# The second feed-forward scatters its results to residual rows, and the next stages' keys, values and masks are prepared ahead of its experts

## The chip, the cores and the metric

One core of a Trainium2 chip runs one launch of the kernel. Its time is the device time of that launch in microseconds (us), median of three runs before the change. TensorE does the matrix products and transposes, VectorE (DVE), ScalarE (ACT) and GpSimd (POOL) the elementwise work. SyncE (SP) issues the plain DMAs and GpSimd the indirect ones, which take their row numbers from a tile.

## The reference

Eight residual blocks follow one another over 4 sequences of 512 rows of 128. The change lies in the fourth, a feed-forward with 8 experts where every row goes to one expert and an expert takes 320 rows at most. The fifth, a relu attention against a context of 77 rows, uses its result.

```python
x = x + _L1_xattn_ref(_layernorm(x, axis=-1), ctx_1024, ctx_1024, ...)
x = x + _L1_ffn_ref(_layernorm(x, axis=-1), L1_ffn_gate_w, L1_ffn_gate_b, L1_ffn_w1, L1_ffn_b1, L1_ffn_w2, L1_ffn_b2)
x = x + _L2_xattn_ref(_layernorm(x, axis=-1), ctx_1024, ctx_1024, mask_1xSxS2_ff0, ...)
...
def _L1_ffn_ref(h, gate_w, gate_b, w1, b1, w2, b2):
    logits = x @ gate_w.T + gate_b
    probs = jax.nn.softmax(logits, axis=-1)
    idx = jnp.argmax(probs, axis=-1)
    top_prob = jnp.max(probs, axis=-1)
    pos = jnp.take_along_axis(jnp.cumsum(one_hot, axis=0), idx[:, None], axis=1)[:, 0] - 1
    keep = pos < capacity
    buf = buf.at[idx, safe_pos].add(x * keep[:, None].astype(x.dtype))
    hdn = jax.nn.relu(jnp.einsum('ecd,edf->ecf', buf, w1) + b1[:, None, :])
    eout = jnp.einsum('ecf,efd->ecd', hdn, w2) + b2[:, None, :]
    gathered = eout[idx, safe_pos]
    out = gathered * (top_prob * keep.astype(x.dtype))[:, None]
```

## The kernel before

The residual stays in SBUF as four tiles `Xb[b]`, one for each sequence (512 rows lie on 128 partitions, 4 blocks of 128 columns). Work is cut into units `i`: units 8 to 11 are the attention of the third block, 12 to 15 that of the fifth, 16 to 19 the feed-forward of the sixth, 20 to 23 the attention of the seventh. Each engine runs its own list of instructions in order; the lists come from the same coroutines, interleaved by `weave` with fractions written by hand. An engine waits on counters (`Signal`) that others raise.

Four routings `route(0)` to `route(3)` are interleaved with units 10 and 11 and what follows. A routing normalizes `Xb[b]` into a tile (`slot[8]` or `slot[9]`, part of `PT`), computes the logits, picks an expert, ranks the rows (two small products with `tri` and `ones`) and writes a slot number into `ints` (L1928); GpSimd then scatters the normalized rows, 512 bytes each, with four indirect DMAs into the DRAM buffer `dbuf` (L2251). VectorE also keeps a second number for the way back and the weight `keep` (L1929 to L1938).

`capacity()` runs the experts. SyncE fetches 320 rows of `dbuf` into one of two buffers (L2366, L2368), TensorE transposes them (L821), VectorE copies the transpose to `OC` (L1944, named `turn1`), four products and their relus (L1370 on ScalarE, L1953 on VectorE) follow, then the second product (`down`). VectorE adds the bias from PSUM into `OT` (L1964 and L1966), and SyncE stores 320 rows in the DRAM buffer `dout` (L2374, L2376). On TensorE the order is: transpose and first product of expert x + 1, second product of x.

After the last expert GpSimd gathers the rows of `dout` for each sequence with four indirect DMAs (L2229), two sequences at once and the others after the square roots of units 12 and 13. VectorE adds gathered row times `keep` to `Xb[b]` (L1536) and starts the layer normalization (L1509, L1514, L1517; GpSimd's reciprocal root L2212; L1522 writes `Ht`); TensorE transposes `Ht` (L507) and the unit goes on: query product, scores, ScalarE's relu L1250, VectorE's mask addition L1641, product with the values, L1644 adds to `Xb`. Beside that stand `l2_prepare` (keys and values of the fifth block), the seventh block's mask (L2167, L2169) and `prepare(a3)`, its keys and values (L1554, L1561, L1575).

At the start `dbuf` is filled with zeros from an SBUF tile (2 stores of 640 KB).

Of the kernel before, what the change touches and what calls it, by code (L numbers as in the profile page):

```python
# [8 lines left out]
F32 = mybir.dt.float32  # L9
# [13 lines left out]
CAP = 320  # L23
# [4 lines left out]
ROW = 257  # L28

# [139 lines left out]
def program(nc, A, out):  # L169
    with ExitStack() as ctx:  # L170
# [34 lines left out]
        PT = sb("PT", 10 * 512)  # L205
# [25 lines left out]
        off1 = sb("off1", 32)  # L231
        ints = sb("ints", 32, I32)
        keep = sb("keep", 16)
# [4 lines left out]
        dbuf = nc.dram_tensor("dbuf", (8 * CAP, 128), F32, kind="Internal").ap()  # L238
        dout = nc.dram_tensor("dout", (8 * CAP, 128), F32, kind="Internal").ap()
# [71 lines left out]
        raws1 = [OT[:, 0:512], OT[:, 512:1024]]  # L311
        outs1 = [OT[:, 1024:1536], OT[:, 1536:2048]]
# [54 lines left out]
        def outputs_at(key, r):  # L367
# [4 lines left out]
            if key[0] % 2 == 0:  # L372
# [9 lines left out]
        ex = [signal("exa", 16), signal("exb", 16)]  # L382
        eo = [signal("eoa", 16), signal("eob", 16)]
        gq = [signal(f"gq{b}", 16) for b in range(NB)]
# [23 lines left out]
        route_, glu, mixed, capV, dve2, d3e, masks, gath = (signal("route"), signal("glu"), signal("mixed"), signal("capV"), signal("dve2"),  # L408
                                                             signal("d3e"), signal("masks"), signal("gath"))
# [7 lines left out]
        def x_at(i):  # L417
            kind, b = units[i]
            if kind == "l0x":
                return ld[f"x{b}"].all()  # L420
            if kind == "l1x":
                return comb.at(b)
            if kind == "l2x":
                return gath.at(b)
            return resid.at(i - 4)
# [57 lines left out]
        def ot_free(key):  # L483
# [6 lines left out]
            return ld["zero"].all() if i == 0 else gath.at(3) if i == 20 else (None, 0)  # L490
# [8 lines left out]
        def tensor(e, w):  # L499
# [287 lines left out]
            def route(b):  # L787
# [4 lines left out]
                for t in range(4):  # L792
                    m = e.transpose(PS[:, k, 128 * t:128 * t + 128], slot[8 + b % 2][:, 128 * t:128 * t + 128], ident[:, :])
# [19 lines left out]
            def capacity():  # L813
                w.wait_ge(*ld["l1f"].all())

                def turn1(x):
                    k, free = banks.take(capV, "x", x)
                    w.wait_ge(*free)
                    w.wait_ge(*ex[x % 2].at(x))
                    for n, (s, c) in enumerate(CP):  # L820
                        m = e.transpose(PS[:, k, s:s + c], raws1[x % 2][0:c, 128 * n:128 * n + 128], ident[0:c, 0:c])  # L821
# [680 lines left out]
        def vector(e, w):  # L1502
# [24 lines left out]
            def norm(i):  # L1527
                kind, b = units[i]
                if kind == "l2x":
                    G = OT[:, 512 * b:512 * b + 512]  # L1530
                    w.wait_ge(*gq[b].all())
                    w.wait_ge(*route_.at("r", b, "w"))
                    w.wait_ge(*resid.at(8 + b))
                    for t in range(4):
                        x = Xb[b][:, 128 * t:128 * t + 128]
                        m = e.scalar_tensor_tensor(x, G[:, 128 * t:128 * t + 128], keep[:, 4 * b + t:4 * b + t + 1], x, ALU.mult, ALU.add)  # L1536
                    m.then_inc(*gath(b))
                    yield
# [335 lines left out]
            def route(b):  # L1874
                H = slot[8 + b % 2]
# [5 lines left out]
                yield from layernorm(Xb[b], H, 2, ("r", b), resid.at(8 + b), sc1[b - 2].all() if b >= 2 else (None, 0))  # L1881
# [3 lines left out]
                L, W8 = v4(R[:, 0:32]), v4(R[:, 32:68])[:, :, 0:8]  # L1885
# [18 lines left out]
                e.reciprocal(P1[:, 4:8], P1[:, 0:4]).then_inc(*route_(*key, 9))  # L1904
# [13 lines left out]
                e.tensor_tensor(C, psl2, v4(off1[:, :]), ALU.add)  # L1918
# [15 lines left out]
                w.wait_ge(*route_.at(*key, "kept"))  # L1934
                kp = keep[:, 4 * b:4 * b + 4]
                e.tensor_reduce(kp, W8, AX, ALU.add).then_inc(*route_(*key, 15))
                w.wait_ge(*route_.at(*key, 15))
                e.tensor_tensor(kp, kp, P1[:, 4:8], ALU.mult).then_inc(*route_(*key, "w"))  # L1938

            def capacity():  # L1940
# [16 lines left out]
                def down(x):  # L1957
                    yield
                    o, k = outs1[x % 2], banks.of(capV, "o", x)
# [4 lines left out]
                    e.tensor_tensor(o[:, 0:256].rearrange("p (t d) -> p t d", t=2), PS[:, k, 0:256].rearrange("p (t d) -> p t d", t=2),  # L1964
                                    bb.rearrange("p (o d) -> p o d", o=1).broadcast_to((128, 2, 128)), ALU.add)
                    e.tensor_tensor(o[0:64, 256:384], PS[0:64, k, 256:384], bb[0:64, :], ALU.add).then_inc(*capV("o", x))  # L1966
# [240 lines left out]
        def gpsimd(e, w):  # L2207
# [14 lines left out]
            def gather(b):  # L2222
                w.wait_ge(*route_.at("r", b, "back"))
                w.wait_ge(*eo[0].all())
                w.wait_ge(*eo[1].all())
                w.wait_ge(*capT.at(7))
                for t in range(4):
                    c = 512 * b + 128 * t
                    e.indirect_dma_start(OT[:, c:c + 128], None, dout,  # L2229
# [3 lines left out]
            def norm(i):  # L2233
                kind, b = units[i]
                if kind == "l2x":
                    yield
# [572 lines left out]
```

## Time and profile before

| | us |
|---|---|
| median of 3 runs | 1205.91 |
| lowest, highest | 1205.54, 1206.64 |
| profiled execution, its own time | 1202.0 |
| its span | 1200.2 |
| TensorE busy | 942.1 (78%) |
| VectorE busy | 609.6 (51%) |
| ScalarE busy | 436.9 (36%) |
| GpSimd busy | 217.0 (18%) |
| mean granted TensorE clock, of full | 0.857 |

The profiled execution lies 0.3% under the median; a difference worked out on its rows is added to the median. Times in rows are microseconds from the start of the span. A row of the timeline merges neighbours of the same kind (x4): its second number runs from the start of the first to the end of the last. What stands in square brackets is the idle time of the engine just before, and what ended it. A GpSimd row of an indirect DMA shows the building of descriptors, the data move later.

### The profile page before, as it was taken

The page shows a single profiled execution, that of the slowest core. Times are in us where ns is not written, and L with a number is a line of the kernel's source. Part 1 is how long each engine was busy: PE and PEld are TensorE (multiplying, and loading weights), DVE is VectorE, ACT ScalarE, POOL GpSimd, SP SyncE. Part 2 cuts the span into 40 slices and gives each one's busy share as a digit, 9 for nine tenths or more (in the row PEclk, how much of TensorE's full clock was granted, in tenths as well). Part 3 has the DMA queues.
Part 4 walks back from the last instruction along what each step waited for, and adds up shares of the span by engine and source line. Part 5 has one row for each costly group of instructions (what it writes and reads, how often), then busy time and mean ns, then how long its engine had stood idle before and what let it go on. Part 6 is the DMA issues. An engine that isn't in the chain of part 4 may idle for free.

```text
span 1200.2 us, 15387 instructions
## 1 busy us (share of the span) xinstructions
PE 942.1 (78%) x5738; PEld 507.2 (42%) x5738; DVE 609.6 (51%) x1637; ACT 436.9 (36%) x750; POOL 217.0 (18%) x214
## 2 busy tenths in 40 slices
PE   4777866597767677479389888887989899888888
PEld 2334444364323333257256423333334334344656
DVE  5344653233545443423553443447687777772534
ACT  2333323142233223011132233233676676565233
POOL 1100050504142101200621010011010000200444
PEclk8889887798978667689689888896999899898999
DMA  9600001212036100011200100000000000102030
GB/s 289 230 1 1 1 28 43 68 54 79 22 121 193 34 1 7 23 42 45 55 2 7 36 1 1 1 1 1 2 1 2 1 1 2 36 2 67 32 91 17
DMA packets 41200, 49.18 MB, mean 41 GB/s; under 512 B 5817, under 2 KB 30674, under 8 KB 40488
## 3 DMA queue, kind: packets, MB, share of 16 engines
q1 hardware_dynamic: 36328, 39.15, 10.6%
q0 software_dynamic: 4800, 9.05, 2.5%
q8 instruction: 47, 0.77, 0.3%
q14 instruction: 25, 0.20, 0.1%
HBM read 33.47 MB, written 19.82 MB: 44 GB/s over the span
## 4 chain that ended last, share of the span: by engine, by line
PE 57%; DVE 20%; issue 10%; ACT 5%; POOL 3%; another core or an unknown queue 2%; DMA 2%; SPq 1%; POOLq 0%; DVEq 0%; ACTq 0%
PE PS L181 50%; DVE KB L2018 4%; DVE KB L1618 3%; PE PS L647 3%; DVE st L1509 1%; POOL OT L2229 1%; DVE Ht L1522 1%; POOL d L2304 1%; DVE OT L1661 1%; POOL ve L2212 1%; PE PS L1122 1%; PE PS L766 1%; ACT KB L1416 1%; ACT PT L1272 1%
## 5 line engine op out<-in xcount | busy, mean ns | idle before, releaser
L2018 DVE TENSOR_REDUCE KB<-PS 128x2 fp32r<-128x1024 f32 x128 | 154.6, 1221 | 49.7 <-PE PS L181 48.4
L1272 ACT ACTIVATE PT<-PS 77x512 f32<-77x512 f32 x192 | 98.0, 590 | 178.3 <-PE PS L181 169.3
L181 PE MATMUL PS<-CX 32*77 32x512 f32 (+2 forms) x896 | 129.7, 595 | 18.2 <-DVE OT L1661 7.3
L2212 POOL TENSOR_TENSOR ve<-ve,nh 128x4 f32<-128x4 f32 x40 | 41.6, 1039 | 482.4 <-DVE ve L1517 480.9
L1618 DVE TENSOR_REDUCE KB<-PS 128x16 fp32r<-128x1232 f32 x48 | 69.1, 1439 | 67.8 <-PE PS L181 67.8
L181 PE MATMUL PS<-RA,RB 128*128 x152 | 87.7, 661 | 9.0 <-issue 4.2
L1436 ACT ACTIVATE PT<-PS 128x1024 f32<-128x1024 f32 x74 | 75.6, 1023 | 37.7 <-PE PS L181 34.1
L181 PE MATMUL PS<-QB,KB 64*128 64x512 f32 x256 | 61.2, 475 | 20.6 <-DVE KB L2018 18.2
L181 PEld LDWEIGHTS PS<-CX 32*128 32x128 f32 (+1 forms) x896 | 47.6, 194 | 64.8 <-issue 20.3
L181 PE MATMUL PS<-PT,VB 77*32 77x512 f32 x384 | 61.2, 715 | 14.8 <-issue 6.1
L181 PE MATMUL PS<-KB,QB 64*128 64x512 f32 x256 | 67.2, 526 | 4.7 <-DVE KB L2018 2.6
L181 PE MATMUL PS<-PT,RB 128*32 128x256 f32 x592 | 62.3, 419 | 0.7 <-ACT PT L1436 0.6
L181 PE MATMUL PS<-KB 32*77 32x512 f32 x192 | 54.8, 998 | 0.0
L1839 DVE TENSOR_TENSOR OT<-OT,PS 128x256 f32<-128x256 f32 x46 | 19.3, 419 | 65.4 <-ACT OT L1327 54.3
L181 PE MATMUL PS<-RB,PT 128*128 128x128 f32 (+2 forms) x352 | 48.2, 296 | 4.8 <-DVE PT L1641 3.7
L181 PEld LDWEIGHTS PS<-RB,PT 128*128 128x128 f32 (+2 forms) x352 | 45.1, 199 | 12.0 <-issue 5.8
L181 PE MATMUL PS<-HT,S 128*128 128x512 f32 x56 | 37.9, 774 | 13.7 <-DVE KB L1618 7.9
L1327 ACT ACTIVATE OT<-PS 128x256 f32<-128x256 f32 x46 | 17.6, 383 | 85.0 <-PE PS L181 63.5
L181 PE MATMUL PS<-RA,PT 128*128 (+1 forms) x304 | 43.2, 289 | 6.7 <-issue 2.6
L181 PEld LDWEIGHTS PS<-QB,KB 64*128 64x128 f32 x256 | 25.9, 199 | 45.1 <-DVE KB L2018 30.7
L181 PEld LDWEIGHTS PS<-KB,QB 64*128 64x128 f32 x256 | 25.7, 199 | 43.8 <-issue 28.7
L2314 POOL DMA_INDIRECT RB<-o,ints x32 | 32.3, 1008 | 65.4 <-DMA o<-CX 56.5
(296 smaller groups left out, 1653.0 us busy)
## 6 DMA issues: line engine op xcount, KB each, us to landing
d<-d SPq DMA_DIRECT2D x2, 1472.0 KB, 11.0
RB<-d SPq DMA_DIRECT2D x10, 256.0 KB
o<-CX SPq DMA_DIRECT2D x10, 256.0 KB, 2.4
RA<-in_l_w SPq DMA_DIRECT2D x1, 2304.0 KB, 10.5
RB<-d SPq DMA_DIRECT2D x4, 514.0 KB
d<-OT SPq DMA_DIRECT2D x2, 1024.0 KB, 7.0
RB<-in_l_w SPq DMA_DIRECT2D x1, 2048.0 KB
RA<-in_l_w SPq DMA_DIRECT2D x1, 2048.0 KB, 15.4
```

Of the source, the lines that this page charges most:

```text
L181: return e.matmul(o, l, r, start=first, stop=last, skip_group_check=True)
L647: m = e.transpose(PS[:, k, 128 * hg:128 * hg + 128], outputs_at(key, hg)[:, 128 * j:128 * j + 128], ident[:, :])
L766: m = e.transpose(PS[:, k, 128 * c:128 * c + 128], hid0[i % 3][:, 128 * c:128 * c + 128], ident[:, :])
L1122: m = e.transpose(PS[:, k, 128 * c:128 * c + 128], slot[i % 3][:, 128 * c:128 * c + 128], ident[:, :])
L1272: e.activation(slot[s][0:NK, :], PS[0:NK, 4 + j, :], ACT.Exp, bias=0.0, scale=a.scale).then_inc(*expd(i, r, j))
L1327: e.activation(hid0[i % 3], PS[:, banks.of(d0e, "h", i), 0:256], ACT.Silu).then_inc(*a0e("s", i))
L1436: e.activation(exps[p].rearrange("p (a n) -> p a n", a=2), PS[:, k:k + 2, :], ACT.Exp, bias=0.0, scale=a4.scale).then_inc(*expd("s", s, c, ...
L1618: e.tensor_reduce(o, PS[:, 0:4, 0:308].rearrange("p i (r k) -> p i r k", k=NK), AX, ALU.max).then_inc(*rmax(i, t))
L1839: e.tensor_tensor(P, P, PS[:, banks.of(d0e, "h", i), 256:512], ALU.mult).then_inc(*d0e("h", i))
L2018: e.tensor_reduce(o, PS[:, k:k + 2, :], AX, ALU.max).then_inc(*rmax("s", s, t, p2))
L2212: e.tensor_tensor(ve[:, 8 * par + 4:8 * par + 8], ve[:, 8 * par:8 * par + 4], nh[:, :], ALU.pow).then_inc(*rstd(*key))
L2314: e.indirect_dma_start(G0[b][n][:, 128 * t:128 * t + 128], None, o0[b // 2], bass.IndirectOffsetOnAxis(ap=ints[:, c:c + 1], axis=0), bound ...
```

## The change

A routing's tile becomes a row of 258 floats: 128 normalized, 128 of the residual (copied by GpSimd), the weight, and the number of the residual row. It is scattered as one row, to `dbuf` with 1032 bytes a row. `dbuf` is filled at the start from a DRAM input of 2.64 MB that carries a row number out of bounds. SyncE stores each `Xb[b]` to a DRAM tensor `x1`. The fetch brings the wide rows into one of four buffers. After the bias, VectorE multiplies by the weight and adds the residual (three instructions an expert); GpSimd scatters the sums to `x1` (three indirect DMAs an expert, 24 in all). When all have landed, SyncE loads `x1` back into `Xb` with four DMAs. The store to `dout`, the 16 gathers and the 16 additions of L1536 go, as do five VectorE instructions of each routing. The masks and `prepare(a3)` stand before the experts on every engine.

```diff
             def route(b):
...
                 e.tensor_reduce(P1[:, 0:4], E, AX, ALU.add).then_inc(*route_(*key, 8))
...
-                e.reciprocal(P1[:, 4:8], P1[:, 0:4]).then_inc(*route_(*key, 9))
+                e.tensor_copy(row1i[b % 2][:, :, 257], off1[:, 32 + 4 * b:36 + 4 * b])
+                e.reciprocal(r[:, :, 256], P1[:, 0:4]).then_inc(*route_(*key, 9))
...
-                e.tensor_scalar(R[:, 444:448], R[:, 440:444], 8.0 * CAP - 1.0, None, ALU.min).then_inc(*route_(*key, 14))
-                w.wait_ge(*route_.at(*key, 14))
-                e.tensor_copy(ints[:, 16 + 4 * b:20 + 4 * b], R[:, 444:448]).then_inc(*route_(*key, "back"))
-                e.scalar_tensor_tensor(W8, psl2, CAP + 0.5, oh1, ALU.is_le, ALU.mult).then_inc(*route_(*key, "kept"))
...
-                e.tensor_reduce(kp, W8, AX, ALU.add).then_inc(*route_(*key, 15))
-                w.wait_ge(*route_.at(*key, 15))
-                e.tensor_tensor(kp, kp, P1[:, 4:8], ALU.mult).then_inc(*route_(*key, "w"))
...
                 def down(x):
...
-                    w.wait_ge(*(eo[x % 2].at(x - 2) if x >= 2 else finT.at(11, 3)))
...
+                    e.tensor_tensor(o[0:64, 2, 0:128], PS[0:64, k, 256:384], bb[0:64, :], ALU.add).then_inc(*capV("o", x))
+                    w.wait_ge(*capV.at("o", x))
+                    for n, (_, c) in enumerate(CP):
+                        e.scalar_tensor_tensor(o[0:c, n, 128:256], o[0:c, n, 0:128], o[0:c, n, 256:257], o[0:c, n, 128:256],
+                                               ALU.mult, ALU.add).then_inc(*capV("r", x, n))
...
-                if kind == "l2x":
-                    yield
                 yield from layernorm(i % 2, (i,))
...
+                e.tensor_copy(r[:, :, 128:256], Xb[b].rearrange("p (t d) -> p t d", t=4)).then_inc(*xrow("r", b))
...
+                    for q in xw:
+                        w.wait_ge(*q.all())
+                    for n, (_, c) in enumerate(CP):
+                        w.wait_ge(*capV.at("r", x, n))
+                        e.indirect_dma_start(x1, bass.IndirectOffsetOnAxis(ap=raws1i[x % 4][0:c, ROW1 * n + 257:ROW1 * n + 258], axis=0),
+                                             raws1[x % 4][0:c, n, 128:256], None, bounds_check=NB * S - 1, oob_is_err=False).then_inc(*eo[x % 4](x, n))
...
+                    w.wait_ge(*(eo[x % 4].at(x - 4, 2) if x >= 4 else finT.at(11, 3)))
...
                 elif name == "capacity":
-                    w.wait_ge(*capV.at("o", 7))
+                    for q in eo:
+                        w.wait_ge(*q.all())
+                    for b in range(NB):
+                        e.dma_start(Xb[b].rearrange("p (t d) -> p t d", t=4), x1[S * b:S * b + S, :].rearrange("(t p) d -> p t d", p=128)).then_inc(*xl[b](b))
...
             weave((route(3), 1))
+            hook("masks")
+            weave((prepare(a3), 6))
             weave((capacity(), 1))
             hook("capacity")
-            hook("gather")
             hook("l2m")
-            hook("masks")
-            weave((norm(12), 6), (l2_prepare(), 6), (prepare(a3), 6))
+            weave((norm(12), 6), (l2_prepare(), 6))
```

VectorE, one expert in the middle of `capacity()`, before:

```order
L1944 COPY OC<-PS 128x320
L1953 TENSOR_SCALAR PT<-PS,b1t 128x320 x2
L1964 TENSOR_TENSOR OT<-PS,S 128x256
L1966 TENSOR_TENSOR OT<-PS,S 64x128
L1944 COPY OC<-PS 128x320
```

The same place after the change:

```order
L1937 COPY OC<-PS 128x320
L1946 TENSOR_SCALAR PT<-PS,b1t 128x320 x2
L1956 TENSOR_TENSOR OT<-PS,S 128x2x128
L1958 TENSOR_TENSOR OT<-PS,S 64x128
L1961 SCALAR_TENSOR_TENSOR OT<-OT 128x128 x2
L1961 SCALAR_TENSOR_TENSOR OT<-OT 64x128
L1937 COPY OC<-PS 128x320
```

Three instructions stand between an expert's bias and the `OC` copy that the next first product reads.

VectorE in units 13 to 15 (fifth block), before; `Ht` is a unit's normalized tile, `PT` the scores with their mask, `X` the residual:

```order
L1514 BN_AGGR mv<-st 128x2 x4
L1517 TENSOR_SCALAR ve<-mv 128x4
L1641 TENSOR_TENSOR PT<-PT,RB 77x512
L1522 TENSOR_SCALAR Ht<-X,mv,ve 128x128 x4
L1644 SCALAR_TENSOR_TENSOR X<-PS,X 128x512
L1536 SCALAR_TENSOR_TENSOR X<-OT,keep,X 128x128 x4
L1509 BN_STATS st<-X 128x6 x4
```

After:

```order
L1524 BN_AGGR mv<-st 128x2 x4
L1527 TENSOR_SCALAR ve<-mv 128x4
L1532 TENSOR_SCALAR Ht<-X,mv,ve 128x128 x4
L1641 TENSOR_TENSOR PT<-PT,RB 77x512
L1644 SCALAR_TENSOR_TENSOR X<-PS,X 128x512
L1519 BN_STATS st<-X 128x6 x4
```

The additions L1536 are gone, and the `Ht` of a later unit has moved ahead of the earlier unit's mask addition.

## Rows read from the trace of the kernel before

**Rows 1.** Stretches: length; busy us of PE, PEld, DVE, ACT, POOL; clock; DMA share, GB/s.

```profile
530.00:569.00 39.00, 36.08 (x229) 29.04 (x228) 12.55 (x29) 6.33 (x12) 0.00 (x0) 1.00 0.18 49
587.60:597.00 9.40, 6.68 (x14) 2.98 (x14) 6.42 (x32) 2.47 (x4) 7.67 (x8) 0.50 0.24 46
700.00:710.00 10.00, 8.15 (x41) 2.78 (x40) 3.57 (x5) 2.95 (x9) 0.00 (x0) 0.83 0.01 2
```

**Rows 2.** Timeline at the end of one expert: start, duration, engine, instruction.

```profile
553.65 0.42 DVE L1964 TENSOR_TENSOR OT<-PS,S 128x256 f32<-128x256 f32 x1 [2.25 <-PE PS L181]
553.99 0.27 DVE L1966 TENSOR_TENSOR OT<-PS,S 64x128 f32<-64x128 f32 x1
554.22 0.49 DVE L1944 COPY OC<-PS 128x320 f32<-128x320 f32 x1
...
554.77 2.42 PE L181 MATMUL PS<-OC,RB 128*128 128x320 f32 x8 [0.58 <-DVE OC L1944]
```

**Rows 3.** Timelines around the ends of routings 0 and 1.

```profile
415.29 1.08 PE L181 MATMUL PS<-PT,VB 77*32 77x512 f32 x4 [0.55 <-DVE KB L1618]
...
451.40 1.94 PE L181 MATMUL PS<-PT,VB 77*32 77x512 f32 x8
...
452.87 0.16 DVE L1929 TENSOR_SCALAR rt<-rt 128x4 f32<-128x4 f32 x1
...
453.66 0.68 DVE L1661 COPY OT<-PS 128x512 f32<-128x512 f32 x1
```

**Rows 4.** Timeline from routing 3's last scatter to the first expert.

```profile
510.11 0.97 POOL L2251 DMA_INDIRECT dbuf<-PT,ints  x1 [0.30 <-issue]
512.44 0.37 SPq L2366 DMA_DIRECT2D OT<-dbuf  x1
...
515.48 0.95 PE L821 MATMUL PS<-ident,OT 128*128 128x128 f32 x3 [11.83 <-DMA OT<-dbuf]
```

**Rows 5.** DMA issues: KB each, median us from issue to landing.

```profile
CX<-d SPq DMA_DIRECT2D x2, 385.5 KB, 3.7
...
OT<-dbuf SPq DMA_DIRECT2D x8, 128.0 KB, 2.3
```

**Rows 6.** Timeline from the seventh expert's bias to unit 12's transpose.

```profile
566.40 0.42 DVE L1964 TENSOR_TENSOR OT<-PS,S 128x256 f32<-128x256 f32 x1 [2.25 <-PE PS L181]
...
580.30 1.14 DVE L1536 SCALAR_TENSOR_TENSOR X<-OT,keep,X 128x128 f32<-128x128 f32 x4 [8.92 <-DMA OT<-dout,ints]
...
584.58 1.28 DVE L1561 MEMSET VB<- 77x1472 f32 x1 [0.24 <-issue]
...
587.58 1.12 PE L507 MATMUL PS<-ident,Ht 128*128 128x128 f32 x4 [15.21 <-DVE VB L1575]
```

**Rows 7.** Timeline of the last block: indirect DMAs and VectorE ahead of them.

```profile
1132.94 1.67 POOL L2279 DMA_INDIRECT d<-VB,ints  x1 [0.30 <-DVE S L2112]
...
1181.42 0.29 DVE L2158 TENSOR_TENSOR PT<-PS,RB 128x128 f32<-128x128 f32 x1 [1.65 <-PE PS L181]
...
1182.51 0.97 POOL L2289 DMA_INDIRECT out<-PT,ints  x1 [1.24 <-DVE PT L2158]
```

**Rows 8.** Timeline of a 256 KB fetch from DRAM, issue and first reader.

```profile
184.56 4.70 SPq L2414 DMA_DIRECT2D RB<-d  x3
...
187.75 1.11 PE L744 MATMUL PS<-ident,RB 128*128 128x128 f32 x4 [6.38 <-DMA RB<-d]
```

**Rows 9.** Timeline of units 14 to 16, the round with the later order.

```profile
605.35 0.69 DVE L1644 SCALAR_TENSOR_TENSOR X<-PS,X 128x512 f32<-128x512 f32 x1
...
608.55 1.11 DVE L1522 TENSOR_SCALAR Ht<-X,mv,ve 128x128 f32<-128x128 f32 x4 [1.12 <-POOL ve L2212]
609.58 0.68 DVE L1641 TENSOR_TENSOR PT<-PT,RB 77x512 f32<-77x512 f32 x1
...
611.94 1.06 PE L507 MATMUL PS<-ident,Ht 128*128 128x128 f32 x4
612.18 0.69 DVE L1644 SCALAR_TENSOR_TENSOR X<-PS,X 128x512 f32<-128x512 f32 x1 [1.93 <-PE PS L181]
```

More of the change, by code:

```diff
@@ L28 @@
 ROW = 257
+ROW1 = 258
 class Signal:
@@ L423, in x_at @@
             if kind == "l2x":
-                return gath.at(b)
+                return xl[b].all()
             return resid.at(i - 4)
@@ L2220, in add_row @@
                 e.tensor_tensor(v, v, r, ALU.add).then_inc(*xrow(*(key if key[0] != "s" else ("y", key[1]))))
[L2222 to L2229, printed above, removed]
-                                         bass.IndirectOffsetOnAxis(ap=ints[:, 16 + 4 * b + t:17 + 4 * b + t], axis=0),
-                                         bounds_check=8 * CAP - 1, oob_is_err=False).then_inc(*gq[b](t))
             def norm(i):
                 kind, b = units[i]
-                if kind == "l2x":
-                    yield
                 yield from layernorm(i % 2, (i,))
@@ L2251, in route, with capacity, down @@
                     e.indirect_dma_start(dbuf, bass.IndirectOffsetOnAxis(ap=ints[:, 4 * b + t:4 * b + t + 1], axis=0),
-                                         H[:, 128 * t:128 * t + 128], None, bounds_check=8 * CAP - 1, oob_is_err=False).then_inc(*sc1[b](t))
+                                         r[:, t, :], None, bounds_check=8 * CAP - 1, oob_is_err=False).then_inc(*sc1[b](t))
                 yield
+            def capacity():
+                def down(x):
+                    yield
+                    for q in xw:
[4 more added lines that the diff above has]
+                                             raws1[x % 4][0:c, n, 128:256], None, bounds_check=NB * S - 1, oob_is_err=False).then_inc(*eo[x % 4](x, n))
+                yield from idle(5)
+                for x in range(8):
+                    if x < 7:
+                        yield from idle(5)
+                    yield from down(x)
             def self_norms(b):
@@ L2358, in maxima, with route @@
                 yield
+            def route(b):
+                yield from idle(5)
+                w.wait_ge(*resid.at(8 + b))
+                e.dma_start(x1[S * b:S * b + S, :].rearrange("(t p) d -> p t d", p=128), Xb[b].rearrange("p (t d) -> p t d", t=4)).then_inc(*xw[b](b))
+                yield
             def capacity():
@@ L2497, in sync @@
                 load("zero0", z[:, 2048:128 * NT0], OT[:, 0:128 * NT0 - 2048])
-            for i in range(2):
-                load("zero", dbuf[1280 * i:1280 * i + 1280, :].rearrange("(p t) d -> p (t d)", p=128), OT[:, 0:1280])
             w.wait_ge(*ld["zero0"].all())
@@ L2504, in sync @@
                 load("zero3", z[:, 128 * NT0:ROW * NT], z0[:, 0:ROW * NT - 128 * NT0])
-            order(nothing, nothing, front, nothing, nothing, nothing, nothing, capacity, nothing, nothing, nothing, nothing, maxima, nothing, nothing,
+            load("zero", dbuf.rearrange("(p t) d -> p (t d)", p=128), A["c_fill"])
+            order(nothing, nothing, front, nothing, nothing, nothing, route, capacity, nothing, nothing, nothing, nothing, maxima, nothing, nothing,
                   nothing, nothing, nothing, experts3, nothing, nothing, nothing, experts0, nothing, hook)
```

102 lines of the change are left out of this document (44 added, 58 removed).

## The prediction

> **What bounds the kernel now.** I read the busy shares first (TensorE 78%), then the busy time by stretch around the fourth block, then the timeline of every place that the change touches. The change lies in three stretches with different limits. In the expert stretch TensorE is busy 36.08 of 39.00 us at the full clock [rows 1], yet each expert ends in a hand-over: TensorE is through, VectorE adds the bias in two instructions, copies the next transpose to `OC`, and only then does the next first product start [rows 2]. So VectorE's list is on the path there for a short piece, six times. In the second stretch, from the last expert to unit 12, TensorE is idle for 15.21 us and the path runs over a store, a gather and a normalization [rows 6]. In the third, units 12 to 15, the path is a round over VectorE, GpSimd and TensorE, and TensorE starts it at half clock (0.50 of full, its 1.2 GHz level, in the first 9.4 us) [rows 1]. From unit 16's transpose at 611.94 us on [rows 9] TensorE is dense again and nothing differs. The sum is therefore the shift of that transpose.
>
> **Start of the kernel.** The fill of `dbuf` grows from 1.3 MB stored to 2.64 MB copied within DRAM. It is now the last DMA in SyncE's start-up list, and its first user is the first scatter at 414 us. I cost it at nothing; uncovered it would have to run ten times longer than any start-up load.
>
> **Routings.** Five small VectorE instructions go from each. In routing 1 they run from 452.87 to 453.66, ahead of the copy L1661, so at most 0.79 us could be won. But the product that the copy reads ends at 453.34 (451.40 + 1.94) [rows 3]; with about 0.1 us of hand-over the copy can move up by 0.23 only. Routing 2 has the same order and I take 0.23 again. In routing 0 they stand ahead of a maximum on which TensorE waits 0.55 us [rows 3]: at most 0.55. The row-number copy costs about 0.09 on the way to the rank product, four times. Sum -1.0 + 0.35 = -0.65 (bounds -1.0 and +0.4). GpSimd's copy of the residual, 128x512, must cost near 1.3 us; it lies in the 10 us and more between GpSimd's root and its scatter, so nothing. SyncE's stores of `Xb` wait for what is done by then, and behind them stand no transfers that are due.
>
> **From routing 3 to the first expert.** Before, the last scatter starts at 510.11, SyncE issues the fetch at 512.44 (2.33 later) and TensorE starts at 515.48 [rows 4]. The fetch of the large piece goes from 128 to 258 KB: by the 2.3 us of the 128 KB transfer and the 3.7 us of one of 385.5 KB with rows nearly as wide [rows 5], about 3.0, so +0.7. The scattered rows are twice as long, for which I add 0.1. Together +0.8. The masks and `prepare(a3)` now stand here. VectorE needs some 4.5 us for them, TensorE 3 at half clock, ScalarE 1.5; all three sit idle from 506 to 515, so they cost nothing unless they hold up GpSimd, who builds the four scatters at this time. Row 1132.94 shows an indirect DMA stretched from 0.97 to 1.67 us while VectorE worked, just before and beside it, on instructions with two SBUF inputs [rows 7], so the bounds are 0.1 and 2.4 (the 0.8, the 0.7 once for the cast and once for the memset, and 0.2).
>
> The Trainium skill, "SBUF — State Buffer", section "SBUF: two separate sides", speaks against this place: a VectorE copy or cast in its two-port mode locks GpSimd out, so that it can't write descriptors until VectorE is done. [...] The trace has no such full stop beside an indirect DMA, only the stretched one above.
>
> **Experts.** Three scalar-tensor-tensor instructions stand between bias and `OC` copy. Four of this form, both inputs in SBUF, take 1.14 us [rows 6], start to start 0.27 each. They first wait for the bias to be written: the two bias instructions end at 554.26 where the copy began at 554.22 [rows 2], and a wait costs 0.03. So 0.07 + 3 x 0.27 = 0.88 us an expert. The copy follows a bias for six of the eight experts (0 to 5): 6 x 0.88 = +5.25. I see nothing that covers it, since TensorE waits on this copy each time [rows 2]; bounds 4.6 (instructions that overlap more) and 6.0. Four buffers instead of two hide the longer fetches and the scatters: a buffer is asked for again four experts later, over 20 us, against 4 us of descriptors, 2.3 of landing and 3 of fetch.
>
> **From the seventh expert to unit 12.** Counted from that expert's bias (566.40 before; unit 12's transpose comes 21.18 us later) [rows 6]. After: bias, wait and first sum 0.99; GpSimd starts 0.80 after its release (1181.71 to 1182.51) [rows 7]; six scatters, those of the last expert queue behind the seventh's, five times 1.27 (0.97 + 0.30) [rows 4] = 6.35; 2.33 from the last start to SyncE's next issue [rows 4]: 10.47. The load of a 256 KB sequence with 512-byte rows: 3.19 from issue to reader [rows 8], 13.66. Then the normalization. Before, the two additions of `l2_prepare`, the normalization and the hand-over took from 581.36 to 587.58, 6.2 us, of which about 1.4 is `prepare(a3)`'s work (its 1.28 memset delays `Ht`, and value copies delay the transpose) [rows 6]: 4.8 remain. Total 18.5, so -2.7. Bounds: -4.0 (the third scatter of an expert has 64 rows and may be cheaper, twice 0.6) and -1.0 (four loads at once slow the first by 1.7).
>
> **Units 12 to 15.** Before, the four transposes from unit 12 to 16 take 24.36 us (587.58 to 611.94) [rows 6, 9]. L1536 goes (1.14 a unit), and no gather stands before GpSimd's roots. But the order changes too: `Ht` of the later unit now precedes the mask addition. The kernel before shows that order once: L1644 at 605.35, next L1644 at 612.18, `Ht` and L1641 between them, a round of 6.83 us [rows 9], of which 0.6 is the values product at half clock. So a round is 6.2 at full clock, hardly less than before. Only the first two are shorter, having no L1644 ahead: 4.0 (normalization alone) and 5.5 (TensorE at half clock: two 128x512 products, transpose, values). 4.0 + 5.5 + 2 x 6.3 = 22.1, and 0.2 for a clock that rises late: 22.3, so -2.1. Bounds -6.9 (rival C) and 0.
>
> **Sum.** -0.65 + 0.8 + 5.25 - 2.7 - 2.1 = +0.6 us, on the median 1206.5. About 0.2% (2.4 us) is what a measurement of this kernel can tell from no change.
>
> **The rivals.** A, the sum: what the experts lose, the two later stretches give back. Terms within their nearer bounds give 1204.0 to 1209.5.
>
> B, the clock falls in the expert stage. TensorE's share there drops from 92% to about 81% with six gaps of 1.5 us. The trace grants only 0.83 in a stretch with 8.15 of 10 us busy [rows 1]. If that held for the experts, 36.08 x (1 / 0.83 - 1) = 7.4 us more, 1213.9. It decides from a mean of 0.95 on (1.9 us, the time then slower than 1208.3). Against it: 1.00 all along before, and gaps far under the idle times after which the clock was seen at half.
>
> C, units 12 to 15 run at the pace of the normalization. If the mask addition of an earlier unit is never waited for, `Ht` can follow `Ht` at 4.2 us (604.32 to 608.55 in that one round [rows 9] has the later start), 4.5 with hand-overs: 4.0 + 3 x 4.5 = 17.5 instead of 22.3, and the time is 1201.7. For it: GpSimd is free. Against: in the order after the change the values product waits behind `Ht`, and the next statistics wait behind its L1644.
>
> D, GpSimd is held up by VectorE, at routing 3's scatters by masks and memset, and at the last experts' scatters by sums with two SBUF inputs: 0.7 for each of two and three scatters [rows 7], 3.5 us, 1210.0. [...]
>
> That the change doesn't do what it says, i.e. that removing the gathers brings nothing, is the -1.0 bound of the fourth term and stands in A.
>
> **How the numbers follow.** A 0.53 (0.41 of it within 0.2%, 0.12 slower), B 0.13, C 0.25 (nearly all faster), D 0.09. Faster 0.25, within 0.2% 0.42, slower 0.33. A alone is 1204.0 to 1209.5. The range 1201.0 to 1211.5 leaves out a third of C (0.08) and the upper part of B (0.10).
>
> **What would show it.** Experts: start to start of `OC` copies 7.26 instead of 6.38 us, clock 1.00 (B: under 0.95). SyncE's first load of `x1` 10.5 us after the seventh expert's bias, unit 12's transpose at 18.5. Unit 12's to unit 16's transpose 22.3 us (C: 17.5). The first expert's transpose 0.5 to 1 us later than 515.48 (D: 2 or more). If the `OC` pitch grows by much under 0.8, or the third stretch shrinks by over 4, the forecast is wrong on the slow side.

## The result and the profile after

| | before | after |
|---|---|---|
| median, us | 1202.45 | 1212.95 |
| lowest, highest | 1189.89, 1206.64 | 1208.06, 1219.77 |
| executions | 11 | 11 |
| profiled execution, its own time | 1202.0 | 1215.7 |
| its span | 1200.2 | 1213.9 |

The changed kernel takes 1.0100 times as long, with a 95% interval of 1.0063 to 1.0137: some 12 us more. I had forecast 1206.5 on a base of 1205.91, no measurable change, and a range up to 1211.5. The time lies outside it.

A table of landmarks, the same event in both profiled executions, says where it happens. The last column is the difference from the line above: what each stretch adds, in the order of the program as far as it has one.

| event | before | after | shift | added in between |
|---|---|---|---|---|
| unit 0, first copy of a values product to `OT` | 46.83 | 57.45 | +10.62 | +10.6 |
| unit 3's transpose | 82.11 | 95.87 | +13.76 | +3.1 |
| routing 0's transpose | 392.89 | 410.31 | +17.42 | +3.7 |
| routing 3's transpose | 495.87 | 510.04 | +14.17 | -3.3 |
| load of the experts' output bias | 491.25 | 505.13 | +13.88 | -0.3 |
| first expert's transpose | 515.48 | 531.11 | +15.63 | +1.75 |
| seventh expert's bias | 566.40 | 588.09 | +21.69 | +6.06 |
| unit 12's transpose | 587.58 | 605.96 | +18.38 | -3.31 |
| unit 16's transpose | 611.94 | 627.13 | +15.19 | -3.19 |
| end of the span | 1200.2 | 1213.9 | +13.7 | -1.5 |

The four stages that the change was about add up to +1.31 us, against +1.25 in my sum. The loss is there before any of them: 10.62 us in the first 58. VectorE's timeline there, after and then before (start, duration, engine, line, instruction; in brackets the idle time ahead and what ended it):

```profile
46.20 0.17 DVE L1527 TENSOR_SCALAR ve<-mv 128x4 f32<-128x4 f32 x1
57.45 0.69 DVE L1661 COPY OT<-PS 128x512 f32<-128x512 f32 x1 [11.08 <-DMA dbuf<-in_c_fill]
```

```profile
46.83 0.69 DVE L1661 COPY OT<-PS 128x512 f32<-128x512 f32 x1 [1.03 <-PE PS L181]
```

The copy used to wait 1.03 us for TensorE. Now it waits 11.08 us for the fill of `dbuf`. SyncE's queue and the chain of waits show the same DMA. Before, from SyncE's timeline:

```profile
25.92 2.48 SPq L2338 DMA_DIRECT2D dbuf<-OT  x2
```

After, the row of the DMA issues (KB, us from issue to landing), then the chain of waits of the first stretch:

```profile
dbuf<-in_c_fill SPq DMA_DIRECT2D x1, 2580.0 KB, 21.1
```

```profile
24.05 8.90 DMA d<-OT
...
36.20 21.12 DMA dbuf<-in_c_fill
57.45 0.70 DVE OT L1661
```

Why does a copy in unit 0 wait for a buffer that the experts use 370 us later? The reason is in `values()`, in a line that the change leaves as it was:

```python
if i == 0:
    w.wait_ge(*ld["zero"].all())
    w.wait_ge(*ld["zero0"].all())
```

Before, the zeros of `dbuf` were stored out of `OT`, so `OT` must not be overwritten until the stores have read it. They were issued from 25.92 on and took 9.2 us, so they had landed long before the copy at 46.83, and the wait cost nothing. Now the fill reads a DRAM constant and no longer touches `OT`, but it still counts on the signal `zero`. It lands at 57.3.

Behind the stop TensorE works at a lower granted clock than before. Windows of after, then of before (length; busy us of PE, PEld, DVE, ACT, POOL; granted clock; DMA share, GB/s):

```profile
57.50:66.00 8.50, 6.35 (x56) 3.29 (x56) 3.80 (x7) 2.53 (x5) 1.27 (x1) 0.70 0.02 8
66.00:80.00 14.00, 10.07 (x50) 3.71 (x50) 2.83 (x3) 3.19 (x6) 0.00 (x0) 0.62 0.00 0
```

```profile
46.00:55.00 9.00, 5.09 (x64) 2.11 (x56) 4.47 (x8) 4.26 (x9) 2.17 (x2) 1.00 0.44 142
55.00:69.00 14.00, 10.76 (x64) 4.51 (x64) 4.33 (x8) 3.73 (x8) 0.00 (x0) 0.76 0.00 0
```

In 22.5 us TensorE gets through 106 products after, at 0.70 and 0.62; in 23 us it got through 128 before, at 1.00 and 0.76. That goes with the 3.1 us between the first two landmarks. But 3.1 us isn't the price of a stop. From the first copy to unit 3's transpose the ten executions without a stop here (before, and all the experiments below but e3 and e10) take 31.69 (e7) to 38.09 us (e9); the three with one take 36.91 (e3), 38.42 (this one) and 43.92 (e10).

Behind routing 3 the trace answers to [rows 4] as follows (timeline of after):

```profile
519.27 1.22 DVE L2163 CAST mkb<-MT 77x2048 bf16<-77x2048 uint8 x1
...
520.51 1.72 POOL L2235 DMA_INDIRECT dbuf<-RY,ints  x1 [11.38 <-issue]
520.64 0.66 DVE L1554 TENSOR_SCALAR CX<-CX,msk 128x308 f32<-128x308 f32 x2
...
521.55 1.28 DVE L1561 MEMSET VB<- 77x1472 f32 x1 [0.25 <-issue]
...
522.54 0.97 POOL L2235 DMA_INDIRECT dbuf<-RY,ints  x1 [0.30 <-issue]
...
527.52 0.36 SPq L2369 DMA_DIRECT2D OT<-dbuf  x1
...
531.11 0.96 PE L831 MATMUL PS<-ident,OT 128*128 128x128 f32 x3 [10.32 <-DMA OT<-dbuf]
```

The first of the four scatters took 1.72 us instead of about 1.05, the fetch 3.6 from issue to reader. The cast had ended at 520.49, before that scatter began, and had not delayed it: with the cast moved away (e6) it starts as late after the bias load, 15.41 us against 15.38. What runs beside its first half are the two L1554, 0.66 us together. The second scatter begins while the memset still runs and takes the usual 0.97. The end of an expert, as [rows 2]:

```profile
573.62 0.42 DVE L1956 TENSOR_TENSOR OT<-PS,S 128x256 f32<-128x256 f32 x1 [2.25 <-PE PS L182]
573.97 0.27 DVE L1958 TENSOR_TENSOR OT<-PS,S 64x128 f32<-64x128 f32 x1
574.27 0.87 DVE L1961 SCALAR_TENSOR_TENSOR OT<-OT 128x128 f32<-128x128 f32 x3
575.07 0.47 DVE L1937 COPY OC<-PS 128x320 f32<-128x320 f32 x1
...
575.60 0.81 PE L182 MATMUL PS<-OC,RB 128*128 128x320 f32 x2 [1.44 <-DVE OC L1937]
```

TensorE is idle for 1.44 us where it was 0.58. The way to unit 12, as [rows 6], and one round of the next units, as [rows 9]:

```profile
588.09 0.43 DVE L1956 TENSOR_TENSOR RX<-PS,S 128x256 f32<-128x256 f32 x1 [2.25 <-PE PS L182]
...
589.86 0.97 POOL L2246 DMA_INDIRECT x<-RX  x1 [3.75 <-DVE RX L1961]
...
598.33 2.01 SPq L2455 DMA_DIRECT2D X<-x  x4
...
601.12 0.87 DVE L1519 BATCH_NORM_STATS2 st<-X 128x6 f32<-128x128 f32 x4 [8.52 <-DMA X<-x]
...
605.96 0.45 PE L517 MATMUL PS<-ident,Ht 128*128 128x128 f32 x1 [13.31 <-DVE Ht L1532]
```

```profile
614.93 0.69 DVE L1644 SCALAR_TENSOR_TENSOR X<-PS,X 128x512 f32<-128x512 f32 x1 [1.25 <-PE PS L182]
...
618.14 1.11 DVE L1532 TENSOR_SCALAR Ht<-X,mv,ve 128x128 f32<-128x128 f32 x4 [1.12 <-POOL ve L2208]
619.17 0.68 DVE L1641 TENSOR_TENSOR PT<-PT,RB 77x512 f32<-77x512 f32 x1
621.10 0.69 DVE L1644 SCALAR_TENSOR_TENSOR X<-PS,X 128x512 f32<-128x512 f32 x1 [1.25 <-PE PS L182]
```

### The profile page after: what moved, and what is told of

It is laid out like the page before. It is cut to its first block, busy times and chain, and to the rows that moved or that the text cites. A ratio compares the mean times of both kernels' runs of the same rounds, so it can differ in the third digit from the quotient of the medians.

```text
span 1213.9 us, 15387 instructions
## 1 busy us (share of the span) xinstructions
PE 943.2 (78%) x5738; PEld 508.4 (42%) x5738; DVE 610.2 (50%) x1629; ACT 437.1 (36%) x750; POOL 225.7 (19%) x226
## 3 DMA queue, kind: packets, MB, share of 16 engines
q1 hardware_dynamic: 37512, 42.61, 11.6%
## 4 chain that ended last, share of the span: by engine, by line
PE 54%; DVE 19%; issue 11%; ACT 4%; DMA 4%; POOL 3%; SPq 2%; another core or an unknown queue 2%; POOLq 0%; DVEq 0%; ACTq 0%
PE PS L182 47%; DVE KB L2014 4%; DVE KB L1618 3%; PE PS L657 2%; SPq L2335 2%; DMA dbuf<-in_c_fill 2%; DVE st L1519 1%; DVE Ht L1532 1%; POOL ve L2208 1%; PE PS L1132 1%; POOL d L2304 1%; DVE OT L1661 1%; DMA d<-OT 1%; ACT KB L1426 1%
## 5 line engine op out<-in xcount | busy, mean ns | idle before, releaser
L182 PE MATMUL PS<-CX 32*77 32x512 f32 (+2 forms) x896 | 133.0, 611 | 28.3 <-DVE OT L1661 17.3
L1661 DVE COPY OT<-PS 128x512 f32<-128x512 f32 x24 | 16.6, 692 | 57.3 <-PE PS L182 46.2
L182 PEld LDWEIGHTS PS<-RA,PT 128*128 128x128 f32 x304 | 40.6, 208 | 8.5 <-issue 8.3
## 6 DMA issues: line engine op xcount, KB each, us to landing
d<-d SPq DMA_DIRECT2D x2, 1472.0 KB, 10.5
dbuf<-in_c_fill SPq DMA_DIRECT2D x1, 2580.0 KB, 21.1
```

The costliest lines, as they stand in the source:

```text
L182: return e.matmul(o, l, r, start=first, stop=last, skip_group_check=True)
L1661: e.tensor_copy(outputs_at((i,), r), PS[:, 0, :]).then_inc(*otc(i, r))
```

## Experiments on the start

The theory: the overlooked wait is nearly the whole difference. Its rival: the 2.58 MB themselves slow other transfers. A second rival: a late start is made up for later, and the loss comes from the experts. The experiments ran later, in three groups: e1 to e4 on the chip numbered 2, e5 to e8 on number 0, e9 to e11 on number 12; the number of the first timing's chip is not recorded. In each group the kernel before takes 1166 us instead of 1202, most of it (26 us) saved between 232 and 303 us, in a stretch that the change leaves alone; why is not known. So ratios are taken only against the kernel before of the same group, and landmarks are compared among these runs.

**e1, the wait taken away.**

```diff
                 if i == 0:
-                    w.wait_ge(*ld["zero"].all())
                     w.wait_ge(*ld["zero0"].all())
```

> The changed kernel with one line less: VectorE's first copy of unit 0's values product into OT no longer waits for the fill of dbuf (it still waits for the stores out of OT; the scatters of the routings still wait for the fill). Theory T (that wait): the copy moves from 57.45 us back to 46.8 to 47.5, unit 3's transpose from 95.87 back to 82 to 83, and the time falls by 12 to 14 us from the changed kernel's, to a ratio of 0.999 to 1.003 against the kernel before (the rest of my sum is +0.6 to +1.3 us). Rival S (the 2.58 MB copy itself slows the transfers and the engines around it, wait or no wait): the copy moves up, but the transposes of units 1 to 3 stay late by 5 us or more, and the ratio stays at 1.006 or above. Rival R (the start-up is made up for later, and the loss is in the experts or behind them): the ratio stays at 1.008 to 1.012 although the start is as before.

Measured: ratio 1.0017 (0.9982 to 1.0051). VectorE's timeline:

```profile
47.13 0.69 DVE L1660 COPY OT<-PS 128x512 f32<-128x512 f32 x1 [1.03 <-PE PS L182]
```

Unit 3's transpose comes at 81.41, though the same 2.58 MB are under way. The wait was the cause, and what is left of the change is not to be told from nothing.

**e2, the wait kept, the fill issued earlier**, ahead of SyncE's wait for the zero stores:

```diff
+            load("zero", dbuf.rearrange("(p t) d -> p (t d)", p=128), A["c_fill"])
             w.wait_ge(*ld["zero0"].all())
...
-            load("zero", dbuf.rearrange("(p t) d -> p (t d)", p=128), A["c_fill"])
```

> The changed kernel, wait kept, with the fill issued by SyncE ahead of its wait for the zero stores instead of last, some 12 us earlier (36.2 to about 24 us). Theory T: only the landing counts. It comes at 45 to 52 us (24 plus 21.1, some more for sharing with the zero stores and copies), the first OT copy at 47 to 52, so 0 to 5 us are left of the 10.6: ratio 1.000 to 1.005. Rival S: the bytes are the same and now compete with the loads that unit 0 and 1 need, so no gain, ratio 1.009 to 1.014.

Measured: 1.0008 (0.9982 to 1.0035). The fill goes out at 25.41 and takes 16.3 us instead of 21.1, in spite of its neighbours (the copies of zeros behind it take 14.2 instead of 10.5), so it lands before the copy wants it:

```profile
25.41 1.06 SPq L2335 DMA_DIRECT2D dbuf<-in_c_fill  x1
```

```profile
47.98 0.69 DVE L1661 COPY OT<-PS 128x512 f32<-128x512 f32 x1 [1.04 <-PE PS L182]
```

The first copy is 0.85 us later than in e1, which is no more than e9 shows with e1's start-up list (48.08). Moving the transfer does what removing the wait does.

**e3 and e4, the same transfer added to the kernel before**, to a DRAM tensor that nobody reads, with and without somebody waiting for it. e3 (e4 counts on a signal `dummy` instead of `zero`):

```diff
+            load("zero", dfill.rearrange("(p t) d -> p (t d)", p=128), A["c_fill"])
             order(nothing, nothing, front, ...
```

> The kernel before plus one DMA at the end of SyncE's start-up list: 2.58 MB copied from one DRAM tensor to another that nobody reads, counted on the signal for which the first OT copy waits. Theory T and rival S: first OT copy at 56 to 60 us instead of 46.83, ratio 1.009 to 1.013 (10 to 14 us for the wait and TensorE's start from half clock behind it). Rival R: the start is late by 10 us but the end by less than 4, ratio under 1.004.

> As the run before it, the same 2.58 MB copy at the same place, but counted on a signal for which nobody waits. Theory T: nothing is late, first OT copy at 46.8 to 48, ratio 0.998 to 1.002. Rival S: as with the wait, ratio 1.006 to 1.013, since the bytes are the same.

Measured: e3 1.0154 (1.0119 to 1.0188), e4 1.0011 (0.9988 to 1.0034). First copies of e3 and of e4:

```profile
59.55 0.69 DVE L1662 COPY OT<-PS 128x512 f32<-128x512 f32 x1 [13.39 <-DMA dfill<-in_c_fill]
```

```profile
46.56 0.69 DVE L1662 COPY OT<-PS 128x512 f32<-128x512 f32 x1 [1.03 <-PE PS L181]
```

One DMA and one wait, with nothing else of the change, slow the kernel before by at least as much as the whole change does: 1.0154 against 1.0100, with intervals that overlap (e3's fill lands 2 us later than the change's, behind the two stores). The same bytes without the wait cost nothing. Both rivals fall. e4 also serves below as the picture of the kernel before.

**e10, the changed kernel once more.**

> The changed kernel as it is, on the chip on which the first experiments ran (it was timed on another, where both kernels take some 35 us more). If the overlooked wait is the whole difference between it and the first experiment: 12 to 17 us above that one, ratio 1.010 to 1.016 against the kernel before, first OT copy at 57 to 60 us. If the chip matters for it: under 1.006.

Measured: 1.0119 (1.0082 to 1.0157), 1179.32 us against 1165.09 of e1: 14 us for one wait, give or take some 6 by the two intervals. First copy at 58.69, after 12.18 us of waiting. (The expectation takes this for the chip of e1. By the numbers it is another; the kernel before takes 1165.9 us on both.) The copy comes 11.6 us later than in e1. In the profiled executions unit 3's transpose is later by 21.2 us (102.61 against 81.41), with a granted clock of 0.55 instead of 0.90 over the 35 us behind the copy. So the wait's own length is steady, and what follows it is not.

## Experiments on the rest of the sum

All of these are the changed kernel without the wait (e1) with one edit more, unless said otherwise. The stages are read from the traces, since most are smaller than the interval of a ratio.

**e5, the sums behind the copy.** For experts 0 to 5 the three L1961 instructions stand behind the `OC` copy of the next transpose instead of ahead of it:

```diff
                     if x < 7:
-                        yield from turn1(x + 1)
+                        ...
+                        e.tensor_copy(xts1[(x + 1) % 2][:, 0:CAP], ...)
+                        if x >= 1:
+                            sums(x - 1)
```

> The changed kernel without the overlooked wait (as in the first run), and with the three weighted sums of the experts 0 to 5 moved in VectorE's list from behind the bias to behind the following copy of the next expert's transpose. Theory P (the sums are paid because they stand ahead of that copy): from copy to copy 6.38 us as in the kernel before, instead of 7.24; the copies of the eight experts span 44 to 45 us instead of 50.4; 5 to 7 us less than the first run, ratio 0.995 to 0.998. Rival Q (the sums cost VectorE's time wherever they stand, they only hold up the next hidden layer's copies): 6.9 to 7.3 us from copy to copy, no gain. The single longer step (8.9 us, one product of 4.1 instead of 2.4 us) that the changed kernel has in this stage should be gone if the 1.44 us gaps of TensorE bring it, and stay if not.

Measured: 0.9931 (0.9901 to 0.9960), faster than both kernels. The hand-over in e5:

```profile
512.39 0.42 DVE L1955 TENSOR_TENSOR RX<-PS,S 128x256 f32<-128x256 f32 x1 [2.25 <-PE PS L182]
512.74 0.27 DVE L1957 TENSOR_TENSOR RX<-PS,S 64x128 f32<-64x128 f32 x1
512.97 0.49 DVE L1974 COPY OC<-PS 128x320 f32<-128x320 f32 x1
...
513.37 0.86 DVE L1965 SCALAR_TENSOR_TENSOR RX<-RX 128x128 f32<-128x128 f32 x3
513.51 2.42 PE L182 MATMUL PS<-OC,RB 128*128 128x320 f32 x8 [0.58 <-DVE OC L1974]
```

Idle 0.58 us again, the sums run beside the product. From the first to the eighth `OC` copy, windows of e1 and of e5:

```profile
483.74:534.14 50.40, 41.03 (x221) 31.29 (x221) 19.43 (x52) 7.39 (x14) 14.32 (x15) 0.92 0.17 46
```

```profile
488.21:532.10 43.89, 39.69 (x221) 30.41 (x221) 18.37 (x48) 7.38 (x14) 14.29 (x15) 0.95 0.20 52
```

6.5 us less, of which 6 x 0.86 = 5.2 are the sums' place and 1.7 is a single step of 8.92 instead of 7.24 us, less 0.3 in the first step. The long step stands in the traces of e1, e2, e7 and of the changed kernel's first timing (there a product of 4.1 us instead of 2.4). It is missing in e5, but in e6, e9 and e10 as well, which have the sums in their old place and take 48.94, 48.59 and 48.68 us. Against these e5 wins about 5 us.

**e6, masks, keys and values back behind the experts** (the two lines `hook("masks")` and `prepare(a3)` in their old place).

> As the first run, with the masks, keys and values of the next stage moved back behind the experts, as in the kernel before. My term: the first scatter of routing 3 goes from 1.72 to about 1.04 us and the fetch is issued 0.7 us earlier, counted from the load of the expert's output bias; behind the experts unit 12's transpose comes 1 to 2 us later (19 to 20 instead of 17.9 after the seventh expert's bias). Sum +0.3 to +1.3 us against the first run, ratio 1.000 to 1.003. Rival L (VectorE's copies hold up GpSimd in full, as the Trainium skill's page SBUF — State Buffer has it in its section on the two sides): the fetch is issued 2.5 us earlier and the sum is about -1.

Measured: 1.0041 (1.0019 to 1.0063). Routing 3's first scatter, e1 and e6:

```profile
472.56 1.72 POOL L2234 DMA_INDIRECT dbuf<-RY,ints  x1 [11.40 <-issue]
```

```profile
474.53 1.06 POOL L2234 DMA_INDIRECT dbuf<-RY,ints  x1 [11.41 <-issue]
```

The fetch is issued 21.88 us after the bias load instead of 22.42: the new place cost 0.54, not 2.5. Unit 12's transpose comes 20.80 after the seventh expert's bias instead of 18.26, so 2.5 us later. More than half of that is GpSimd, held up in the scatters of the last expert, where the cast now stands:

```profile
544.18 2.34 POOL L2245 DMA_INDIRECT x<-RX  x1 [0.30 <-DVE RX L1960]
544.29 1.21 DVE L2162 CAST mkb<-MT 77x2048 bf16<-77x2048 uint8 x1
545.43 0.30 DVE L2164 TENSOR_SCALAR negI<-ident 77x308 bf16<-77x308 f32 x1
```

The scatter takes 2.34 us instead of 0.97, 1.37 more, beside two VectorE instructions that last 1.44 from the start of the first to the end of the second. By the Trainium skill's page "SBUF — State Buffer", section "SBUF: two separate sides", a VectorE copy or cast in its two-port mode locks GpSimd out until it has ended. This trace agrees. The 2.5 us of rival L, cast and memset together, are not paid in the new place: the cast ends there before the first scatter begins (520.49 against 520.51 in the changed kernel), and the scatter that begins beside the memset is not stretched. What the new place pays, 0.66 us on one scatter, fits the length of the two L1554; no run moves these two alone.

Units 12 to 16 take 22.45 instead of 21.19, but e9 and e10, with everything in the new place, take 22.36 and 22.34, so this part can't be put down to the old place. The long step in the experts is absent here (-1.7). Over the whole stretch from the bias load to unit 16 it is 123.98 against 122.22, +1.8, a little more than I expected. The ratio is above my range, but its interval overlaps e1's.

**e7, `Ht` behind the mask addition again** (one `yield` ahead of the normalization of units 12 to 15, on VectorE and on GpSimd).

> As the first run, with the normalization of units 12 to 23 held back by one step on VectorE and GpSimd, so that the mask addition stands ahead of Ht again. If this order sets the round (my step on units 12 to 15): the four transposes from unit 12 to 16 take 17.5 to 19.5 us instead of 21.2, ratio 2 to 3 us lower, 0.998 to 1.000. If the round is set by TensorE's own work and the hand-overs: 20.8 to 21.8 us, no change. If holding back the start of the normalization costs more than the order gives: 22 us or more, ratio 1.002 and up.

Measured: 0.9966 (0.9939 to 0.9992). The transposes from unit 12 to 16 take 19.78 us instead of 21.19, and unit 12 itself comes 1.16 earlier. But the next three units give 2.26 back. Windows from unit 16 to 19, e1 and e7:

```profile
579.38:611.78 32.40, 31.57 (x152) 23.16 (x151) 14.24 (x49) 9.16 (x13) 7.25 (x7) 0.84 0.01 2
```

```profile
577.29:611.95 34.66, 34.66 (x152) 25.95 (x152) 14.32 (x49) 9.17 (x13) 7.23 (x6) 0.76 0.01 1
```

TensorE works without a pause there, at a clock of 0.76 instead of 0.84. The order was part of the round's 6.2 us (my step holds), and at unit 19 only 0.3 us of the gain is left. So these stages don't explain why the ratio lies below my range (0.998 to 1.000); its interval just overlaps e1's. e8 repeats both figures: 19.78 us from unit 12 to 16, 34.63 from 16 to 19.

**e8, e5 and e7 together.**

> The edits of the two runs before last and last but one together: sums later and Ht behind the mask addition, without the overlooked wait. If both gains exist and add: 7 to 9 us less than the first run, ratio 0.992 to 0.996. If only the sums' place counts: 0.995 to 0.998, as the run with that alone.

Measured: 0.9923 (0.9897 to 0.9949). (The expectation calls e7 and e5 "the two runs before last and last but one".) Not to be told from e5 alone: only the place of the sums counts for sure.

**e9 and e11, the five small instructions of routing 0.** From routing 0's transpose to routing 1's the changed kernel takes 3.3 us less than the kernel before, in every trace (40.4 against 43.6). e9 puts the five back into e1's routing 0; e11 takes them out of the kernel before's routing 0 and runs them in routing 1.

```diff
                 e.tensor_copy(ints[:, 4 * b:4 * b + 4], R[:, 440:444]).then_inc(*route_(*key, "slot"))
+                if b == 0:
+                    e.tensor_scalar(R[:, 444:448], R[:, 440:444], 8.0 * CAP - 1.0, None, ALU.min)...
+                    ...
```

> As the first run (changed kernel without the overlooked wait), with the five small VectorE instructions of the old routing put back in routing 0 alone, ahead of the maximum L1618; their results go to scratch. In the traces so far the time from routing 0's to routing 1's transposes is 43.6 us in all of the kernel before and 40.4 in all of the changed one, with TensorE's granted clock at 0.65 and 0.75. Theory C (the 0.55 us for which TensorE waits behind these five keeps its clock at half for the next 15 us): 43.6 us again, 3.3 more than the first run. Rival (the instructions cost what they last): 40.9 to 41.2.

> The kernel before with the same five instructions of routing 0 moved from ahead of the maximum L1618 to routing 1, where ten instead of five stand ahead of the copy L1661. Theory C: 40.3 to 40.6 us from routing 0's to routing 1's transposes instead of 43.6, from routing 1's to 2's up to 0.8 more, so 2.5 to 3.3 us less in all, ratio 0.997 to 0.999. Rival (something else of the change does it, as the scattered rows or SyncE's stores): 43.0 to 43.6.

Measured: e9 1.0036 (1.0005 to 1.0066), e11 0.9985 (0.9961 to 1.0008). Windows from routing 0's to routing 1's transposes, in e1, e9, e4 (the kernel before, as it were) and e11:

```profile
362.36:402.71 40.35, 30.30 (x166) 14.10 (x167) 17.44 (x52) 10.66 (x21) 5.66 (x6) 0.75 0.06 18
```

```profile
366.99:410.87 43.88, 33.36 (x167) 15.74 (x167) 18.32 (x57) 10.65 (x21) 5.65 (x6) 0.66 0.05 16
```

```profile
363.51:407.19 43.68, 33.37 (x167) 15.74 (x167) 18.05 (x56) 10.67 (x21) 5.04 (x5) 0.65 0.02 5
```

```profile
363.80:406.56 42.76, 32.14 (x167) 15.39 (x167) 17.35 (x51) 10.65 (x21) 5.03 (x5) 0.68 0.02 5
```

Five instructions of 0.79 us together cost 3.5 us when put back (e9), with the clock at 0.66 instead of 0.75. TensorE's busy time for the same products grows by 3.1 of it. Five-microsecond windows of e1 and of e9 behind the place show where it falls:

```profile
382.36:387.36 5.00, 4.17 (x25) 1.11 (x18) 2.20 (x3) 2.05 (x4) 3.05 (x3) 0.69 0.15 53
387.36:392.36 5.00, 3.47 (x25) 2.19 (x27) 3.18 (x9) 0.00 (x0) 0.98 (x1) 1.00 0.10 35
```

```profile
386.99:391.99 5.00, 3.91 (x19) 0.48 (x11) 2.81 (x9) 2.04 (x4) 3.05 (x3) 0.50 0.16 56
391.99:396.99 5.00, 4.03 (x16) 2.58 (x16) 1.97 (x6) 0.00 (x0) 0.98 (x1) 0.50 0.10 35
```

e11 is the weaker half of the pair: 0.9 us less in this interval and not 3.3, but 1.4 less in the next and 1.1 less in the third, 99.57 us over the three against 103.02 in e4 and 99.72 in e1. The sum of 3.45 us is there, spread over other places than I said. So the five cause the loss (e9); that the 0.55 us gap alone decides it is not shown, since e11 closed the gap and TensorE still ran at half clock for the ten microseconds behind it.

## Why the prediction was wrong

**Start of the kernel: the step that failed.** I wrote that the first user of the fill "is the first scatter at 414 us" and "I cost it at nothing". The first user was VectorE at 46.83 us. I looked for who reads `dbuf`, not for who waits on the signal `zero`, and I read only the changed lines. The rows for the right sum were at hand. The kernel before wanted the copy at 46.83. In its place in the list the fill could not be issued before the zero copies, about 36 us, and [rows 5] move 385.5 KB in 3.7 us, some 100 GB/s, by which 2580 KB take 25: landing at 61, cost 14. Measured: issue 36.20, 21.1 us, 10.62 us of delay, and 3.1 behind it in this pair of traces, which other traces neither repeat nor exclude (see above); 14 us of time between e10 and e1. The bound that I did give, that the fill "would have to run ten times longer than any start-up load", was a bound for the wrong reader.

**Routings: right in the sign, wrong in the mechanism.** Forecast -0.65 with a bound of -1.0, measured -3.3 for the time between routings 0 and 3. Nearly all of it lies between routings 0 and 1, where TensorE is busy for 30.32 us instead of 33.34, at a clock of 0.75 instead of 0.65. I had priced the five instructions by their own length; e9 shows that they cost several times that. The row-number copy and SyncE's stores cost nothing that shows. GpSimd's copy of the residual took 0.60 us, not 1.3, and was hidden.

**Routing 3 to the first expert: mechanism right, size off.** +1.75 against +0.8, inside the bounds (0.1 to 2.4). The fetch came out as costed, 3.59 from issue to reader instead of 3.04, +0.55 where I had +0.7. Missing were the stretched first scatter, 0.7 (e6: the masks' place costs 0.54 in all), and 0.4 ahead of it, from the bias load to the first scatter (15.38 against 14.97). I had named cast and memset as what could stretch a scatter. The cast ends before the first one, the memset stretches none, and the 0.66 us fits two instructions L1554 that my bounds don't name. The trace before had no full stop beside an indirect DMA, as I wrote, but e6 has one, of 1.37 us.

**Experts: right in mechanism.** 0.86 an expert against 0.88; +6.06 against +5.25 in all, just over my bound of 6.0. The rest is one long step (+1.7) and a first step 0.8 shorter. e5 shows that the cost was the place of the sums, as the step said.

**Seventh expert to unit 12: right in mechanism and size.** 17.87 against 18.5: the load of `x1` goes out 10.24 us after the bias (10.5), its reader starts 2.79 later (3.19), and the normalization takes 4.84 (4.8). -3.31 against -2.7.

**Units 12 to 15: right in the mechanism, one us off.** 21.17 against 22.3. The rounds took 6.2 as forecast (614.73, 620.90, 627.13), the first two 3.70 and 5.07 instead of 4.0 and 5.5. e7 and e8 show that the order costs 1.4 of it. Rival C, the pace of the normalization, did not come.

**The four stages together: in part luck.** +1.31 us against +1.25 looks like a hit, but the single misses are +0.95, +0.81, -0.61 and -1.09 and cancel.

**The rivals.** B came in part: the clock over the experts was 0.93, under the 0.95 that I had given as its sign, but from one dip that cost 1.7 us, and not 7.4. The same gaps stand in e6, e9 and e10, and there the dip is absent, so the gaps alone do not bring it. D came in part: 0.66 at one scatter, nothing at the experts' scatters, though the sums stand there. None of the rivals spoke of the start.

**What stays open.** Between unit 3 and routing 0 the changed kernel lost another 3.7 us in the first traces, and 1.5 came back behind unit 16, in stretches that the change does not touch. The same stretch from unit 3 to routing 0 takes 277.7 to 283.7 us in the eleven later traces, whichever kernel it is, so such differences are no sign of the change. The granted clock differs there between executions, and I have not separated it. Nor is it settled what decides whether the experts have the long step, and whether units 16 to 19 run at 0.84 (e1, 32.40 us) or at 0.70 (e10, 36.08 us).

## What to carry to other kernels

When an edit makes a transfer longer, search for every wait on its signal, in unchanged lines too, and compare the new landing time with the earliest of them. A wait that guards a source buffer outlives the buffer: once the transfer reads something else, the wait can go. Work that an engine adds beside a hand-over costs its full length if it stands ahead of the hand-over, and here cost nothing behind it (e5: 0.86 us an expert, about 5 us in all; e5 and e8, which have this edit, beat both kernels clearly). When VectorE work is moved next to indirect DMAs of GpSimd, compare the start and end of each VectorE instruction with the scatters: the same cast cost nothing when it ended just ahead of a scatter, and most of 1.37 us beside one (e6).

## What the runs showed of the hardware

- Five VectorE instructions of 0.79 us put back in one place cost 3.5 us (e1 and e9), 3.1 of it as longer busy time of TensorE, whose granted clock was 0.50 of full for ten microseconds where it was 0.69 and 1.00.
- The work from the first copy to unit 3's transpose took 36.9, 38.4 and 43.9 us behind a stop of 11 to 13 us, and 31.7 to 38.1 us without one; in the first pair of traces the granted clock was 0.70 and 0.62 behind the stop where it had been 1.00 and 0.76.
- An indirect DMA's scatter took 2.34 us instead of 0.97 on GpSimd beside a VectorE cast of 1.21 us and the 0.30 us instruction behind it (e6), and 1.72 beside two TENSOR_SCALAR of 0.66 us together (the changed kernel). One that began beside a memset of 1.28 us took 0.97.
- A DRAM to DRAM copy of 2580 KB took 21.1 us issued at 36.20 (20.4 to 23.0 in the other runs that issue it there), and 16.3 us issued at 25.41 beside 2.9 MB of stores (e2).
- The same kernel took 1202 us in the first timing and 1166 us on each of three chips later; the change's ratio came out alike (1.0100 and 1.0119).
